# The scatters of counts beside the third graph layer's product wait for that product's progress

## The chip, the cores and the metric

The kernel runs on one core of a Trainium2 chip. The metric is the time of one execution on the device in microseconds, the median of several runs. One more execution was taken with the hardware profiler on; its trace is what the rows below come from.

## What is computed

A network of four layers over a graph with 3125 nodes of 256 features and 53125 edges (25000 random pairs in both directions and one loop per node, sorted by target). Each layer is a graph operation and a feed-forward one, both added to x. Cut to what this case touches:

```python
# third graph layer: aggregation with edge weights
h = x @ weight_l
msgs = edge_val[:, None] * h[edge_col]
agg = segment_sum(msgs, edge_row, num_segments=3125)
out = agg + bias_l + x @ weight_r + bias_r

# fourth graph layer: two graph convolutions over the same edges
s, d = concatenate([src, loop]), concatenate([dst, loop])
dinv = rsqrt(segment_sum(ones_like(d), d, num_segments=3125))
out = segment_sum((x @ W)[s] * (dinv[s] * dinv[d])[:, None], d, 3125) + b
```

## The kernel before

The layers run one after the other. Each is made of blocks; in a block the five engines have a program each, and no engine starts the next block before all have finished the last. Nodes are kept in 26 tiles of 128, edges in 416 tiles of 128 (`ET`).

The third and fourth graph layers do their segment sums as products with a dense matrix. For that, two tables in device memory are filled edge by edge long before they are read: `edge_weights` (f32, by `place_weights`, L150) with the weights for the third layer, and `edge_counts` (bf16, by `place_counts`, L141) with the number of repeats of an edge for the fourth. A tile of 128 edges is one indirect DMA that GpSimd issues and that writes 128 single elements to computed addresses, a scatter. At most four scatters of a table are in flight: each has one of four semaphores (`LANES`, L136), and a scatter waits until the one four before it has landed. The scatters are spread by hand over the blocks in which GpSimd has little to do; `COUNTED` (L831) says how many counts are placed by the end of which block:

```python
COUNTED = (97, 302, 336, 348, 374)
```

Counts 0 to 96 are placed in the feed-forward block before, 97 to 301, that is 205 scatters, in the block `weighted_products` (L2770), 302 to 335 in the block after it, `layer2_sums` (L2870), the others later. Nobody reads `edge_counts` before the fourth graph layer.

Some scatters of weights are issued by `place_weights_beside` (L159), which makes scatter t wait for a semaphore of the block's product first, so that the scatters are spread over it: those in the first feed-forward layer (L872) and in the second graph layer's sum.

`weighted_products` multiplies the normalized nodes with the matrix of weights. TensorE walks over a list `order` of 56 steps, `(h, s)`: two halves of the target nodes, and 28 slices of 128 sources in each. In a step it does 8 matmuls (L2841) of 128 rows by 391 columns in f32, 2 halves of the features by 4 pieces of the targets, one for each bank of PSUM; a bank collects over the 28 slices of a half and is copied out by ScalarE (L2856) at the end of it. Only the last matmul of a step increments the semaphore `used`. SyncE loads the 782 KB of weights of a step (L2794) into one of six buffers and waits on `used` for a free one. The sources' slices 25 to 27 beyond the nodes' own tiles come from four gathers that GpSimd issues first (L2824), after the table of nodes has been stored. VectorE and ScalarE normalize the nodes in the block's first 15 us (`StepNorm`) and then have next to nothing to do.

In the trace each f32 matmul of this block leaves two records of matmul and two of weight load.

Of the kernel before, what the change touches and what calls it, by code (L numbers as in the profile page):

```python
# [135 lines left out]
def landed(eng, lanes, t):  # L136

    eng.wait_ge(lanes[t % LANES], 16 * (t // LANES + 1))


def place_counts(nc, g, pool, lo, hi):  # L141

    for t in range(lo, hi):
        if t >= LANES:
            landed(pool, g.counts_in, t - LANES)
        nc.gpsimd.indirect_dma_start(g.counts, bass.IndirectOffsetOnAxis(ap=g.cell[:, t:t + 1].bitcast(U32), axis=0),  # L146
                                     g.repeats[:, t:t + 1], None).then_inc(g.counts_in[t % LANES], 16)


def place_weights(nc, g, pool, lo, hi):  # L150

    for t in range(lo, hi):
        if t >= LANES:
            landed(pool, g.weights_in, t - LANES)
        nc.gpsimd.indirect_dma_start(g.weights, bass.IndirectOffsetOnAxis(ap=g.share_cell[:, t:t + 1].bitcast(U32), axis=0),  # L155
                                     g.shares[:, t:t + 1], None).then_inc(g.weights_in[t % LANES], 16)


def place_weights_beside(nc, g, pool, lo, hi, signal, first, steps):  # L159

    for t in range(lo, hi):
        pool.wait_ge(signal, first + (t - lo) * steps // (hi - lo))
        place_weights(nc, g, pool, t, t + 1)


def layer_norm(nc, g, table, meanwhile=None, arrived=None):
# [664 lines left out]
COUNTED = (97, 302, 336, 348, 374)  # L831
# [5 lines left out]
def layer0_ffn(nc, g, a, table):  # L837

    scratch = nc.dram_tensor("score_scratch", (ROWS,), F32).ap()
    with ExitStack() as stack:  # L840
# [8 lines left out]
        with ExitStack() as s2:  # L849
# [12 lines left out]
            @block.gpsimd  # L862
            def _(pool):

                nc.gpsimd.affine_select(out=before[:, :], in_=g.ones[:, :], compare_op=ALU.is_gt, fill=0.0, base=0,
                                        pattern=[[-1, P]], channel_multiplier=1).then_inc(passed, 1)

                place_weights(nc, g, pool, 0, PLACED[0])
                for t in range(0, NT):
                    front.normed(pool, t)  # L870
                    nc.gpsimd.tensor_tensor(g.x[:, t, :], g.x[:, t, :], g.xn[:, t, :], ALU.add).then_inc(passed, 1)
                place_weights_beside(nc, g, pool, PLACED[0], PLACED[1], hidden, 5, NF * (ROWS // G))  # L872
# [638 lines left out]
def weighted_sum(nc, g, kept, weight, bias):  # L1511

    with ExitStack() as stack:
# [25 lines left out]
        @block.gpsimd  # L1539
        def _(pool):  # L1540
            nc.gpsimd.memset(no_edges[:, :], 0.0).then_inc(blank, 1)
            for t in range(ST):
                nc.gpsimd.tensor_tensor(g.x[:, t, :], g.x[:, t, :], bias[:, :], ALU.add).then_inc(biased, 1)
            place_weights_beside(nc, g, pool, PLACED[3], PLACED[4], summed, 1, PAIRS)
# [1225 lines left out]
def weighted_products(nc, g, a, table, bias, pairs):  # L2770
# [5 lines left out]
    with ExitStack() as stack:  # L2776
# [3 lines left out]
        stored, listed, fetched, used, done, lifted, numbered, biased, held = (sem(n) for n in (  # L2780
            "rows_stored", "listed", "fetched", "used", "done", "lifted", "numbered", "biased", "held"))
# [4 lines left out]
        first = a.dst_row[1:1 + ET * P].rearrange("(t n) -> t n", n=P)[:, 0:2]  # L2786
        rest = NODES - whole * P
        order = [(h, s) for h in range(2) for s in range(WT)]

        @block.sync  # L2790
        def _(sp):
            def load(i):
                h, s = order[i]
                sp.dma_start(weights[:, i % S, :], by_row[s * P:(s + 1) * P, h * half:(h + 1) * half]).then_inc(loaded[i % S], 16)  # L2794

            for lane in g.weights_in:
                sp.wait_ge(lane, 16 * (ET // LANES))
            for i in range(S):
                load(i)
            for dst, src in pairs:  # L2800
                sp.dma_start(dst, src).then_inc(held, 16)
            sp.wait_ge(numbered, 2)
            sp.dma_start(idx[rest:P, 0, :], first[0:P - rest, :]).then_inc(listed, 16)
            for k in range(1, WT - whole):
                lo = P - rest + (k - 1) * P
                n = min(P, ET - lo)
                sp.dma_start(idx[0:n, k, :], first[lo:lo + n, :]).then_inc(listed, 16)
            norm.normed(sp, norm.BY_ACT - 1)
            norm.normed(sp, NT - 1)
            sp.dma_start(table.rearrange("(t p) d -> p t d", p=P), g.xn[:, :, :]).then_inc(stored, 16)  # L2810
            for i in range(S, len(order)):
                sp.wait_ge(used, i - S + 1)
                load(i)
            sp.wait_ge(held, 16 * len(pairs))

        @block.gpsimd
        def _(pool):
            nc.gpsimd.memset(idx[:, :, :], 0).then_inc(numbered, 1)
            pool.wait_ge(numbered, 1)
            nc.gpsimd.iota(idx[0:rest, 0, :], [[0, 2]], base=whole * P, channel_multiplier=1).then_inc(numbered, 1)  # L2820
            pool.wait_ge(stored, 16)
            pool.wait_ge(listed, 16 * (WT - whole))
            for k in range(WT - whole):
                nc.gpsimd.indirect_dma_start(extra[:, k, :], None, table,  # L2824
                                             bass.IndirectOffsetOnAxis(ap=idx[:, k, 0:1].bitcast(U32), axis=0)).then_inc(fetched, 16)
            place_counts(nc, g, pool, COUNTED[0], COUNTED[1])

        @block.tensor
        def _(pe):
# [581 lines left out]
```

## Time and profile before

| | us |
|---|---|
| median of the timed runs | 3591.89 |
| lowest and highest of three | 3591.84, 3598.81 |
| span of the profiled execution | 4271.3 |
| mean clock granted to TensorE in it | 0.856 |
| block `weighted_products` in it, first matmul to last | 2588.9 to 3104.8 |

The profiled execution takes longer than the timed ones. Times of a row are its own, in us from the span's start. In the rows PE is TensorE's matmuls, PEld its weight loads, DVE VectorE, ACT ScalarE, POOL GpSimd, SP SyncE; PEclk is the granted clock as a share of the full 2.4 GHz, so 0.50 is the lower level, 1.2 GHz. "issue" is idle time for which the profile shows no event that was waited for.

### The profile page before, as it was taken

The numbers are of one execution on the slowest core, as the hardware profiler recorded it, in microseconds if no ns is written. First come the engines' busy times: TensorE is split into PE (matmuls) and PEld (weight loads), VectorE is DVE, ScalarE is ACT, GpSimd is POOL, SyncE is SP. The second block draws the span as 40 slices with busy tenths as digits, with TensorE's granted clock in tenths as the row PEclk, the third lists the DMA queues.
The fourth block names the chain that finished last, engine by engine and source line by source line (L and its number), as shares of the span: only waits on it lengthen the run. The fifth ranks groups of instructions, "written<-read, shape, count | busy, mean of one in ns | idle before, by whom it ended". The sixth has DMA issues, their size and how long they took to land. (4 is left out here: it accounts for less than half of the span.)

```text
span 4271.3 us, 47439 instructions
## 1 busy us (share of the span) xinstructions
PE 3169.9 (74%) x14365; PEld 2194.5 (51%) x14365; DVE 1967.2 (46%) x4724; ACT 1137.9 (27%) x2521; POOL 2014.5 (47%) x2031
## 2 busy tenths in 40 slices
PE   4777777976888888459955886228975885998966
PEld 3565655854444445248843553114553553445856
DVE  5444446924666666899961342000024336023332
ACT  3444441221222222249931110000022221012310
POOL 5666664664555555675555553770035552000032
PEclk9888988987888988669977998558987997999978
DMA  5455452004766766248831225004313114452434
GB/s 176 159 160 160 160 159 94 1 13 142 197 198 192 202 186 199 68 151 271 281 117 63 93 65 197 23 15 136 128 45 128 52 52 141 151 198 86 152 125 137
DMA packets 281656, 563.05 MB, mean 132 GB/s; under 512 B 61793, under 2 KB 184101, under 8 KB 280774
## 3 DMA queue, kind: packets, MB, share of 16 engines
q1 hardware_dynamic: 200070, 404.27, 28.4%
q0 software_dynamic: 81344, 155.76, 13.4%
q8 instruction: 127, 2.08, 0.2%
q14 instruction: 115, 0.94, 0.1%
HBM read 381.99 MB, written 177.86 MB: 131 GB/s over the span
## 5 line engine op out<-in xcount | busy, mean ns | idle before, releaser
L1282 PE MATMUL bank<-layer_gnn_h_nodes,layer_gnn_s_onehot_t 128*128 x1664 | 547.9, 457 | 110.4 <-issue 73.5
L146 POOL DMA_INDIRECT edge_counts<-repeats,count_cell x416 | 408.1, 981 | 360.8 <-SPq L2872 226.5
L155 POOL DMA_INDIRECT edge_weights<-shares,share_cell x416 | 463.5, 1114 | 240.8 <-issue 91.9
L1234 POOL DMA_INDIRECT layer_gnn_s_rows<-gat_rows,src_cols x416 | 401.6, 965 | 355.2 <-DMA kept_rows<-layer_gnn_s_rows 211.3
L527 POOL DMA_INDIRECT layer_gnn_sum_rows<-xn_rows,src_cols x416 | 417.8, 1004 | 199.1 <-issue 110.8
L2841 PE MATMUL bank<-layer_gnn_b_weights,xn_nodes 128*128 128x391 f32 x768 | 300.7, 534 | 205.1 <-issue 173.3
L1282 PEld LDWEIGHTS bank<-layer_gnn_h_nodes,layer_gnn_s_onehot_t 128*128 128x128 f32 x1664 | 317.7, 212 | 208.8 <-issue 135.8
L2841 PEld LDWEIGHTS bank<-layer_gnn_b_weights,xn_nodes 128*128 128x128 f32 x768 | 155.5, 203 | 349.8 <-issue 225.1
L1292 ACT ACTIVATE layer_gnn_s_enc<-bank 128x256 f32<-128x256 f32 x416 | 154.7, 384 | 592.1 <-PE bank L1275 345.7
L590 PE MATMUL bank<-layer_gnn_sum_onehot,layer_gnn_sum_rows 128*128 128x256 f32 x832 | 296.8, 442 | 2.0 <-issue 1.8
L1311 DVE TENSOR_TENSOR layer_gnn_s_mix<-bank,layer_gnn_s_enc 128x256 f32<-128x256 f32 x416 | 176.0, 423 | 257.9 <-PE bank L1282 124.2
L2924 DVE TENSOR_TENSOR x_nodes<-x_nodes,bank 128x256 f32<-128x256 f32 x25 | 10.4, 417 | 556.8 <-issue 501.6
L1554 PE MATMUL bank<-layer_gnn_w_onehot,layer_gnn_w_part 128*128 128x256 f32 x832 | 251.6, 385 | 20.0 <-DVE layer_gnn_w_part L1599 19.8
L3254 PE MATMUL bank<-layer_gnn_gcn_sum_counts,layer_gnn_parts 128*128 128x512 bf16 (+1 forms) x1050 | 226.9, 379 | 8.4 <-DVE layer_gnn_parts L2962 7.1
L615 ACT ACTIVATE layer_gnn_sum_onehot<-layer_gnn_sum_dist,ones 128x384 f32<-128x384 f32 x208 | 126.3, 608 | 321.1 <-remote 182.6
L721 DVE TENSOR_TENSOR edge_sums_turned<-edge_sums_turned,bank 128x512 f32 x208 | 141.7, 681 | 129.3 <-PE bank L591 62.9
L591 PEld LDWEIGHTS bank<-layer_gnn_sum_onehot,layer_gnn_sum_rows 128*128 128x128 f32 x832 | 179.6, 216 | 34.5 <-issue 3.5
L2148 PE MATMUL bank<-layer_ffn_e_w,layer_ffn_e_ht 128*128 128x256 f32 x512 | 127.9, 410 | 69.3 <-DVE layer_ffn_e_y L2204 49.7
L591 PE MATMUL bank<-layer_gnn_sum_onehot,layer_gnn_sum_rows 128*128 128x128 f32 x832 | 178.0, 299 | 1.5 <-issue 1.4
L1303 DVE TENSOR_TENSOR layer_gnn_s_onehot_t<-layer_gnn_s_dst_across,edge_sums 128x256 f32<-128x256 int32 x416 | 172.8, 416 | 4.0 <-DMA layer_gnn_s_edge_attr<-attr_parts 4.0
L553 PE MATMUL bank<-layer_gnn_sum_key_line,layer_gnn_sum_ones 3*128 3x512 bf16 x104 | 43.9, 422 | 173.0 <-DVE layer_gnn_sum_same L684 125.0
L3254 PEld LDWEIGHTS bank<-layer_gnn_gcn_sum_counts,layer_gnn_parts 128*128 128x128 bf16 x1050 | 103.2, 99 | 131.1 <-issue 10.6
(645 smaller groups left out, 6077.7 us busy)
## 6 DMA issues: line engine op xcount, KB each, us to landing
kept_rows<-layer_gnn_s_rows SPq DMA_DIRECT2D x104, 512.0 KB
layer_gnn_w_rows<-kept_rows SPq DMA_DIRECT2D x104, 512.0 KB
edge_weights<-layer_gnn_sum_zeros SPq DMA_DIRECT2D x56, 800.0 KB
layer_gnn_gcn_sum_counts<-edge_counts SPq DMA_DIRECT2D x50, 896.0 KB
layer_gnn_b_weights<-edge_weights SPq DMA_DIRECT2D x56, 782.0 KB
layer_gnn_s_dst_across<-in_dst_row SPq DMA_DIRECT2D x104, 256.0 KB
edge_counts<-layer_gnn_w_no_edges SPq DMA_DIRECT2D x25, 896.0 KB
layer_ffn_e_w<-in_l1f_w SPq DMA_DIRECT2D x16, 1024.0 KB
```

The lines of the kernel that those rows point to most:

```text
L146: nc.gpsimd.indirect_dma_start(g.counts, bass.IndirectOffsetOnAxis(ap=g.cell[:, t:t + 1].bitcast(U32), axis=0), g.repeats[:, t:t + 1], Non ...
L155: nc.gpsimd.indirect_dma_start(g.weights, bass.IndirectOffsetOnAxis(ap=g.share_cell[:, t:t + 1].bitcast(U32), axis=0), g.shares[:, t:t + 1 ...
L527: nc.gpsimd.indirect_dma_start(rows[:, t % U, :], None, table, bass.IndirectOffsetOnAxis(ap=g.srcc[:, t:t + 1].bitcast(U32), axis=0)).then ...
L590: nc.tensor.matmul(sums(p)[:, c, :], rows[:, t % U, c * P:(c + 1) * P], onehot[:, p % 4, P:3 * P], start=True, stop=False)
L591: last = nc.tensor.matmul(sums(p)[:, c, 0:P], rows[:, (t - 1) % U, c * P:(c + 1) * P], onehot[:, p % 4, 0:P], start=False, stop=True)
L1234: nc.gpsimd.indirect_dma_start(rows[:, t % U, :], None, htable, bass.IndirectOffsetOnAxis(ap=g.srcc[:, t:t + 1].bitcast(U32), axis=0)).the ...
L1282: last = nc.tensor.matmul(g.ps[4 + t % 4][:, 0:D + HEADS], onehot_t[:, t % 4, k, :], hflat[:, ds(w * AW + (k * AW + HEADS), D + HEADS)], s ...
L1303: nc.vector.tensor_tensor(onehot_t[:, t % 4, :, :], dst[:, t // Q % PARTS, t % Q * P:(t % Q + 1) * P].unsqueeze(1).to_broadcast([P, 2, P]) ...
L1311: nc.vector.tensor_tensor(mix[:, t % 4, :], g.ps[4 + t % 4][:, 0:D], enc[:, t % 4, :], ALU.mult).then_inc(mixed, 1)
L1554: nc.tensor.matmul(sums(p)[:, c, :], part[:, p % 4, 1, c * P:(c + 1) * P], onehot[:, p % 4, P:3 * P], start=True, stop=False)
L2841: last = nc.tensor.matmul(g.ps[4 * c + j][:, 0:w], rows, weights[:, i % S, j * w:(j + 1) * w], start=(s == 0), stop=(s == WT - 1))
L3254: last = nc.tensor.matmul(g.ps[b][:, 0:cells(b)], parts[:, k, s * P:(s + 1) * P], counts[:, s % S, b * 512:b * 512 + cells(b)], start=(s = ...
```

## The change

A new function `place_counts_beside` does for the counts what `place_weights_beside` does for the weights, and `weighted_products` calls it in place of `place_counts`:

```diff
+def place_counts_beside(nc, g, pool, lo, hi, signal, first, steps):
+
+    for t in range(lo, hi):
+        pool.wait_ge(signal, first + (t - lo) * steps // (hi - lo))
+        place_counts(nc, g, pool, t, t + 1)
@@ weighted_products, @block.gpsimd
-            place_counts(nc, g, pool, COUNTED[0], COUNTED[1])
+            place_counts_beside(nc, g, pool, COUNTED[0], COUNTED[1], used, 4, len(order) - 6)
```

`used` is the semaphore of finished steps, `len(order) - 6` is 50. So the first scatter waits until 4 steps of the product are done, and the last of the 205 until 4 + 204 x 50 // 205 = 53 are. The other lines of the program, and the order of instructions on every engine, stay as they are (line numbers behind the new function grow by 7).

On GpSimd this is where the scatters start in `weighted_products`, before:

```order
L2820 IOTA layer_gnn_b_idx 53x2 [waits layer0_gnn_sum_gathered3]
L2824 DMA layer_gnn_b_extra<-xn_rows,layer_gnn_b_idx 128x256 [waits layer0_gnn_ln_scaled,layer0_gnn_ln_normed]
L2824 DMA layer_gnn_b_extra<-xn_rows,layer_gnn_b_idx 128x256 x3
L146 DMA edge_counts<-repeats,count_cell 11468800x1 [waits counts_in1]
L146 DMA edge_counts<-repeats,count_cell 11468800x1 [waits counts_in2]
L146 DMA edge_counts<-repeats,count_cell 11468800x1 [waits counts_in3]
L146 DMA edge_counts<-repeats,count_cell 11468800x1 [waits counts_in0]
```

and after (a semaphore that is used again under another name is printed with its first name; `layer0_gnn_sum_gathered0` is `used` here):

```order
L2827 IOTA layer_gnn_b_idx 53x2 [waits layer0_gnn_sum_gathered3]
L2831 DMA layer_gnn_b_extra<-xn_rows,layer_gnn_b_idx 128x256 [waits layer0_gnn_ln_scaled,layer0_gnn_ln_normed]
L2831 DMA layer_gnn_b_extra<-xn_rows,layer_gnn_b_idx 128x256 x3
L146 DMA edge_counts<-repeats,count_cell 11468800x1 [waits counts_in1,layer0_gnn_sum_gathered0]
L146 DMA edge_counts<-repeats,count_cell 11468800x1 [waits counts_in2,layer0_gnn_sum_gathered0]
L146 DMA edge_counts<-repeats,count_cell 11468800x1 [waits counts_in3,layer0_gnn_sum_gathered0]
L146 DMA edge_counts<-repeats,count_cell 11468800x1 [waits counts_in0,layer0_gnn_sum_gathered0]
```

Nothing has moved; each scatter of the block has one more semaphore to wait for.

## Rows read from the trace of the kernel before

**Rows 1.** The page: span, and TensorE's busy tenths and clock in 40 slices.
```profile
span 4271.3 us, 47439 instructions
...
PE   4777777976888888459955886228975885998966
...
PEclk9888988987888988669977998558987997999978
```

**Rows 2.** Busy time by stretches, columns in the first line, x counts instructions.
```profile
core 0: us, PE busy (x) PEld busy (x) DVE busy (x) ACT busy (x) POOL busy (x), PEclk, DMA share, GB/s
50.00:650.00 600.00, 439.58 (x2730) 356.33 (x2730) 289.47 (x538) 278.08 (x628) 402.47 (x409) 0.87 0.50 160
1050.00:1750.00 700.00, 588.82 (x1989) 338.82 (x1989) 459.18 (x1624) 147.98 (x398) 375.93 (x390) 0.87 0.68 194
...
2589.00:2657.00 68.00, 68.00 (x200) 38.91 (x201) 17.99 (x54) 6.73 (x14) 31.79 (x34) 0.97 0.69 240
2657.00:2902.00 245.00, 72.13 (x91) 25.51 (x90) 0.00 (x0) 0.00 (x0) 168.40 (x176) 0.51 0.08 20
2902.00:3105.00 203.00, 202.37 (x606) 115.22 (x606) 0.00 (x0) 7.64 (x16) 0.00 (x0) 0.99 0.42 135
...
750.00:900.00 150.00, 144.82 (x658) 126.49 (x658) 109.07 (x197) 46.89 (x105) 93.50 (x97) 0.98 0.02 1
```

**Rows 3.** TensorE's timeline in the product: start, length, what, idle before and releaser.
```profile
start us, us, engine line op out<-in xcount [idle before <-releaser]
2588.86 68.36 PE L2841 MATMUL bank<-layer_gnn_b_weights,xn_nodes 128*128 128x391 f32 x200 [31.82 <-DMA layer_gnn_b_weights<-edge_weights]
...
2682.62 0.81 PE L2841 MATMUL bank<-layer_gnn_b_weights,xn_nodes 128*128 128x391 f32 x1 [1.99 <-issue]
2685.42 0.81 PE L2841 MATMUL bank<-layer_gnn_b_weights,xn_nodes 128*128 128x391 f32 x1 [1.99 <-issue]
...
2902.42 33.83 PE L2841 MATMUL bank<-layer_gnn_b_weights,xn_nodes 128*128 128x391 f32 x94 [0.59 <-issue]
...
2957.15 126.56 PE L2841 MATMUL bank<-layer_gnn_b_weights,xn_nodes 128*128 128x391 f32 x384
3083.55 21.23 PE L2841 MATMUL bank<-layer_gnn_b_weights,layer_gnn_b_extra 128*128 128x391 f32 x64
```

**Rows 4.** GpSimd's timeline beside the product: the first scatter, and the last two.
```profile
2618.08 0.99 POOL L146 DMA_INDIRECT edge_counts<-repeats,count_cell  x1 [0.30 <-issue]
...
2877.50 0.96 POOL L146 DMA_INDIRECT edge_counts<-repeats,count_cell  x1 [0.30 <-issue]
2878.76 0.96 POOL L146 DMA_INDIRECT edge_counts<-repeats,count_cell  x1 [0.30 <-issue]
```

**Rows 5.** TensorE's timeline in the block after it, from 3122 on.
```profile
3133.73 0.47 PE L2888 MATMUL bank<-identity,xn_nodes 128*128 128x128 f32 x1
3136.53 0.37 PE L2888 MATMUL bank<-identity,xn_nodes 128*128 128x128 f32 x1 [2.33 <-issue]
3139.33 0.59 PE L2899 MATMUL bank<-layer_gnn_wl,edge_sums_turned 128*128 128x256 f32 x1 [2.42 <-issue]
3141.43 0.59 PE L2899 MATMUL bank<-layer_gnn_wl,edge_sums_turned 128*128 128x256 f32 x1 [1.51 <-issue]
...
3154.52 2.07 PE L2899 MATMUL bank<-layer_gnn_wl,edge_sums_turned 128*128 128x256 f32 x4
```

**Rows 6.** DMA queues from 2580 to 3110: packets, MB, share of 16 engines.
```profile
q8 instruction: 7, 0.11, 0.1%
```

**Rows 7.** The page's groups: the gathers of the first graph layer.
```profile
L527 POOL DMA_INDIRECT layer_gnn_sum_rows<-xn_rows,src_cols x416 | 417.8, 1004 | 199.1 <-issue 110.8
```

**Rows 8.** GpSimd's timeline, paced scatters of weights in the first feed-forward layer.
```profile
807.94 0.96 POOL L155 DMA_INDIRECT edge_weights<-shares,share_cell  x1 [0.30 <-issue]
811.65 1.00 POOL L155 DMA_INDIRECT edge_weights<-shares,share_cell  x1 [2.76 <-PE bank L901]
812.96 0.95 POOL L155 DMA_INDIRECT edge_weights<-shares,share_cell  x1 [0.30 <-issue]
```

## The prediction

> **What bounds the kernel now.** I began with the page: the profiled execution spans 4271.3 us, the three timed runs have a median of 3591.89 us, so the profiled one is 679 us longer. That gap has to be kept in mind through everything below. The reader is to see two digits in the page's slices [rows 1]: slices 26 and 27 are the only ones in which TensorE is under 30% busy at the lower of its two clocks while vector and scalar engines do nothing at all. They lie in the third graph layer's product, and that is where the change works. No engine bounds the whole span; stage follows stage behind barriers, so only this stage's end matters.
>
> I then read busy time by stretches [rows 2]. From 2589 to 2657 TensorE is 100% busy, from 2902 to 3105 again (202.4 of 203 us). Between, from 2657 to 2902, it has 91 matmul records in 245 us. The product's timeline shows how [rows 3]: one record every 2.8 us, each put down to "issue", that is, waiting for nothing the profile can see; before and after, a step of the product (8 matmuls, 16 records) takes 126.56 / 24 = 5.27 us, or 21.23 / 4 = 5.31 us. GpSimd's timeline beside it [rows 4]: 205 scatters of counts from 2618.08 to 2878.76, one every 1.26 us, hardly ever waiting. The slow pace begins 39 us after the first scatter and ends about 23 us after the last. The same thing happens once more: with the 34 scatters of the next block TensorE falls to one record in 2.1 to 2.8 us from 3122 on, and returns to full pace at 3154.5 [rows 5]. So scatters at GpSimd's full rate and a slow TensorE go together in the profiled execution. Unslowed, the product would have ended at 2588.9 + 56 x 5.27 = 2884.0; it ended at 3083.55 + 21.23 = 3104.8. The stretch costs **221 us of the profiled span**. The whole case turns on one question: does a timed run pay it too?
>
> **Is the slow stretch in the timed runs?** Against: (a) The pace does not depend on the work. A record of 391 columns, of 256 and of 128 all come 2.8 us apart [rows 3, 5], and nothing in the program ties a single matmul to a scatter: only the eighth of a step increments a semaphore. A contention for data would scale with columns. (b) Data can't be short: the DMA engines are 8% busy there (20 GB/s) and TensorE waits for its weights once, at the start [rows 2, 3]. The instruction queue fetched 7 packets with 0.11 MB over the stage, about 64 B for each of its 1792 matmul and weight-load records, so nothing is fetched twice [rows 6]. What is left is something paid per instruction, and keeping a record of each instruction and each transfer is what only the profiled execution does. (c) The 679 us must come from somewhere. In the stretches I can bound, little can go: the first layer's gathers cannot go below 409 x 1.26 = 515 of 600 us (85 to gain), the edge scores not below TensorE's 589 of 700 (111), the first feed-forward layer not below 145 of 150 (5) [rows 2, 7]. With 2902 to 3105 (nothing to gain) that makes 201 us in 1653. If the slow stretch counts as extra, the other 2373 us have to give 679 - 201 - 221 = 257 us, 11%; if it is in the timed runs too, they have to give 478 us, 20%. The first is easier to believe. (d) GpSimd's scatters end at 2879.7, just inside the unslowed product's 2884.
>
> For: the profile shows no record being waited for, and (c) uses GpSimd's 1.26 us as a floor, of which 0.30 are "issue" and may themselves be the profile's.
>
> The Trainium skill's page "SBUF — State Buffer" (section "SBUF: two separate sides") says that engine ports and DMA ports are apart and that a DMA and a compute operation can't slow each other. The trace can neither confirm nor refute the rule for these scatters; by it, pacing them frees nothing in a timed run, 0 us, which speaks against a gain from this change.
>
> **The change, part by part.** Nothing is added to compute or to move; the same 205 scatters stand in the same order on GpSimd's queue, each with one more semaphore to wait for: scatter i of 205 waits until 4 + (50 i) // 205 steps are done.
> - *Do the waits bind in a timed run?* Steps take 5.27 us, so the schedule lets 4.1 / 5.27 = 0.778 scatters pass per us; GpSimd's own rate is 1 / 1.26 = 0.794. At the first scatter (2618.08) (2618.1 - 2588.9) / 5.27 = 5.5 steps are done, where the schedule asks for 4, so it starts 8 scatters behind the limit and gains 0.016 x 258 = 4 in the whole phase. The waits hardly ever bind. If a timed run's GpSimd is quicker (0.96 us, the busy part alone), they do: then the scatters end when step 53 does, 2588.9 + 53 x 5.27 = 2868, plus 4 scatters, 2873: still 11 us inside the product. Nothing is queued behind them on GpSimd but the block's end, and nobody reads the counts before the last graph layer. Cost 0.
> - *What does a wait that is already met cost?* The scatters of shares in the first feed-forward layer have just such a wait each, and come 1.26 us apart like those without [rows 4, 8]. Under 0.01 us each, 205 x 0.01 = 2 us, covered by the 4 us by which GpSimd ends ahead of the product. Cost 0; without that cover 2 us.
> - *What does TensorE gain?* In the timed runs between 0 and 221 us. I take 0, by (a) to (c).
> - *The other 34 scatters* (next block) keep their place and rate. 0.
>
> Sum for the timed runs: 0, so 3591.9, and I put 3591 for it. In the **profiled** execution the waits do bind once TensorE slows: GpSimd then stops with it, and TensorE gets the gaps. The nearest row is the paced stretch from 750 to 900: 97 scatters and 658 records in 150 us, TensorE 145 us busy at clock 0.98 [rows 2]: 0.65 scatters per us leave 4.4 records per us untouched. Here it would be up to 0.78 per us beside 3.0 records. I expect steps of 5.3 to 6.3 us, 56 x 5.3 to 6.3 = 297 to 353 us in place of 516, so a profiled span shorter by 160 to 220 us, while the median stays.
>
> **Rivals.**
> 1. *The timed runs have the whole slow stretch.* Then the gain above is real: 3592 minus 160 to 220 is 3372 to 3432, say 3400. For it: the trace shows the slowdown plainly and no cause in the recording. Against: (a) to (c). 0.17. The Trainium skill's page "NOTIFIC — the notification-queue block" (section "10. Constraints, capacities, measured rates") says that emitting an instruction's record costs the engine zero cycles, which would make the stretch real and the time this rival's; its section "7.1 Overflow" knows a mode in which a full queue stalls the engine that writes, which would make it the profile's own, and the time my forecast's. No row tells the two apart.
> 2. *The timed runs have a part of it.* GpSimd's flood slows semaphores or issue a little without records too. Of 221 us, 5 to 25% is 11 to 55 us: 3537 to 3581. 0.09.
> 3. *Slower: the added wait lengthens each scatter.* It decides from the point at which 205 scatters overrun the product, (2884 - 2879.7) / 205 = 0.02 us each. If the gap of 0.30 us became 0.40, the phase would end 205 x 0.10 - 4 = 16 us after the product: 3608; if it doubled, 205 x 0.30 - 4 = 57 us: 3649. Against it stand the paced scatters at 1.26 us [rows 8]. 0.10, with smaller overruns beside it.
> 4. *The change does nothing even in the profile*: the limit lies 8 scatters ahead and the rate is 98% of the old one. TensorE slows as before, but then the limit is reached within some 10 scatters, so I give this little weight; the timed runs would stay at 3592 all the same. It is inside the forecast.
>
> **How the numbers follow.** About 0.2% (7 us) is what a measurement of this kernel can tell from no change; the three runs themselves are 3591.84 to 3598.81. Forecast 3591, within 0.2%: 0.62 (with rival 4). Rival 1 0.17, rival 2 0.09, and 0.02 for a small gain from an unseen overlap: faster 0.28. Rival 3 with its smaller forms: slower 0.10. The range runs from 3540 (most of rival 2) to 3608 (rival 3 at 0.10 us more per scatter); it leaves out rival 1 and the long overruns, 0.2 together.
>
> **What would show it right or wrong.** In the changed kernel's profile: records in the product about 0.33 us apart throughout, few or no "issue" waits of 2 us, the product's length 297 to 353 us, scatters still 1.26 us apart within a burst with waits for TensorE between bursts, the last one before the product's end; the stretch from 3122 to 3154 just as slow as now, only earlier. If the profiled span falls by some 200 us and the median by nothing, the slow stretch was the profile's own. If both fall by as much, step (a) to (c) is wrong and rival 1 right. If scatters are further apart than 1.26 us inside a burst and the block ends with GpSimd, it is rival 3.

## The result, and the profile after

The changed kernel takes 3605.3 us (11 runs, 3599.1 to 3608.4), the kernel before beside it 3595.5 us (11 runs): ratio 1.0031, 95% interval 1.0023 to 1.0039. It is slower by 9.8 us between the medians, by some 11 us (8 to 14) by the ratio. The forecast was 3591 us and no change. Two executions of the kernel before that took far longer than all others beside them (4465.3 and 7233.8 us, clocks 0.763 and 1.0) enter no ratio.

One thing has to be said before any row is read. The kernel before was seen at two levels in this study: on chips 5, 10 and 14 and beside the result (that chip is not on record) the medians of its timed runs are 3592 to 3596 us, on chips 0 and 7 they are 4274 and 4303 us. I call these the short and the long level. The trace read ahead of the prediction (4271.3 us) shows the long level, the timed runs beside it the short one. The trace of the changed kernel shows the short one (3600.4 us), so its difference to rows 1 to 5 is mostly not the change. A second trace of the kernel before at the short level, taken as the first experiment, is what it has to be read against.

The page of the changed kernel: span, TensorE's busy tenths and its clock in 40 slices, as in [rows 1].

```profile
span 3600.4 us, 47644 instructions
...
PE   4887887996999999079977987998589859999696
...
PEclk9999998997999999589988998999789979999898
```

The same lines of the kernel before at the short level:

```profile
span 3593.7 us, 47439 instructions
...
PE   4878877995999999179986986999589869999696
```

There is no stretch of TensorE under 30% in the product (slices 25 to 28 here) any more, but there is none in the kernel before either. What differs is the end of the block. TensorE's timeline, the product's last stretches and the next block's first matmuls, in the changed kernel ([rows 3] are the like):

```profile
start us, us, engine line op out<-in xcount [idle before <-releaser]
2181.65 128.08 PE L2848 MATMUL bank<-layer_gnn_b_weights,xn_nodes 128*128 128x391 f32 x384 [37.39 <-DMA layer_gnn_b_weights<-edge_weights]
...
2457.03 21.23 PE L2848 MATMUL bank<-layer_gnn_b_weights,layer_gnn_b_extra 128*128 128x391 f32 x64
2493.87 1.94 PE L2895 MATMUL bank<-identity,xn_nodes 128*128 128x128 f32 x8 [15.60 <-PEq L2783]
```

and in the kernel before at the short level:

```profile
2183.78 128.88 PE L2841 MATMUL bank<-layer_gnn_b_weights,xn_nodes 128*128 128x391 f32 x384 [38.23 <-DMA layer_gnn_b_weights<-edge_weights]
...
2459.97 21.23 PE L2841 MATMUL bank<-layer_gnn_b_weights,layer_gnn_b_extra 128*128 128x391 f32 x64
2486.21 1.94 PE L2888 MATMUL bank<-identity,xn_nodes 128*128 128x128 f32 x8 [5.00 <-PEq L2776]
```

The product itself is as long in both (296.6 and 297.4 us). TensorE then waits 5.00 us for the next block in the one and 15.60 in the other. GpSimd's timeline tells why. Changed kernel, the block's first scatter, its last, and the next block's first ([rows 4] are the like):

```profile
2210.93 0.99 POOL L146 DMA_INDIRECT edge_counts<-repeats,count_cell  x1 [0.30 <-issue]
...
2484.80 0.95 POOL L146 DMA_INDIRECT edge_counts<-repeats,count_cell  x1 [0.31 <-issue]
2494.47 0.96 POOL L146 DMA_INDIRECT edge_counts<-repeats,count_cell  x1 [8.72 <-SPq L2879]
```

Kernel before, short level:

```profile
2213.07 0.99 POOL L146 DMA_INDIRECT edge_counts<-repeats,count_cell  x1 [0.30 <-issue]
...
2477.14 0.96 POOL L146 DMA_INDIRECT edge_counts<-repeats,count_cell  x1 [0.30 <-issue]
2486.82 0.95 POOL L146 DMA_INDIRECT edge_counts<-repeats,count_cell  x1 [8.72 <-SPq L2872]
```

In both, TensorE's first matmul of the next block comes 9.07 us after the start of GpSimd's last scatter (2493.87 - 2484.80, 2486.21 - 2477.14). That fits a block that GpSimd ends, in the kernel before too, though its last scatter starts 4 us before the product is over; two runs below try it. And the 205 scatters take 2484.80 - 2210.93 = 273.9 us with the change and 2477.14 - 2213.07 = 264.1 us without it: 9.8 us, as much as the medians differ.

### The profile page after: what moved, and what is told of

The parts are those of the page before. It is cut to its first block and busy times, and to the rows that moved or that the text cites. A ratio compares the mean times of both kernels' runs of the same rounds, so it can differ in the third digit from the quotient of the medians.

```text
span 3600.4 us, 47644 instructions
## 1 busy us (share of the span) xinstructions
PE 2979.0 (83%) x14365; PEld 2110.7 (59%) x14365; DVE 1972.7 (55%) x4724; ACT 1154.6 (32%) x2521; POOL 2015.6 (56%) x2031
## 3 DMA queue, kind: packets, MB, share of 16 engines
q0 software_dynamic: 81344, 155.76, 15.4%
## 5 line engine op out<-in xcount | busy, mean ns | idle before, releaser
L1289 PE MATMUL bank<-layer_gnn_h_nodes,layer_gnn_s_onehot_t 128*128 x1664 | 484.4, 414 | 0.9 <-DVE layer_gnn_s_onehot_t L1310 0.2
L597 PE MATMUL bank<-layer_gnn_sum_onehot,layer_gnn_sum_rows 128*128 128x256 f32 x832 | 276.9, 416 | 97.2 <-DMA layer_gnn_sum_rows<-xn_rows,src_cols 86.9
L1289 PEld LDWEIGHTS bank<-layer_gnn_h_nodes,layer_gnn_s_onehot_t 128*128 128x128 f32 x1664 | 283.3, 190 | 79.7 <-issue 4.0
L2848 PE MATMUL bank<-layer_gnn_b_weights,xn_nodes 128*128 128x391 f32 x768 | 254.6, 493 | 37.4 <-DMA layer_gnn_b_weights<-edge_weights 37.4
L1561 PE MATMUL bank<-layer_gnn_w_onehot,layer_gnn_w_part 128*128 128x256 f32 x832 | 250.1, 382 | 15.1 <-DVE layer_gnn_w_part L1606 14.5
L2848 PEld LDWEIGHTS bank<-layer_gnn_b_weights,xn_nodes 128*128 128x128 f32 x768 | 146.0, 190 | 145.7 <-DMA layer_gnn_b_weights<-edge_weights 37.8
L597 PEld LDWEIGHTS bank<-layer_gnn_sum_onehot,layer_gnn_sum_rows 128*128 128x128 f32 x832 | 134.8, 202 | 124.3 <-issue 81.7
L2931 DVE TENSOR_TENSOR x_nodes<-x_nodes,bank 128x256 f32<-128x256 f32 x25 | 10.5, 421 | 324.5 <-PE bank L2909 324.5
L598 PEld LDWEIGHTS bank<-layer_gnn_sum_onehot,layer_gnn_sum_rows 128*128 128x128 f32 x832 | 168.0, 202 | 25.9
L1562 PEld LDWEIGHTS bank<-layer_gnn_w_onehot,layer_gnn_w_part 128*128 128x128 f32 x832 | 158.7, 191 | 21.6
L609 ACT ACTIVATE layer_gnn_sum_dist<-iota_row,ayer_gnn_sum_minus_local 128x128 f32<-128x128 f32 (+1 forms) x416 | 166.0, 447 | 13.8 <-DVE ayer_gnn_sum_minus_local L631 7.9
```

The lines of the kernel that those rows point to most:

```text
L597: nc.tensor.matmul(sums(p)[:, c, :], rows[:, t % U, c * P:(c + 1) * P], onehot[:, p % 4, P:3 * P], start=True, stop=False)
L598: last = nc.tensor.matmul(sums(p)[:, c, 0:P], rows[:, (t - 1) % U, c * P:(c + 1) * P], onehot[:, p % 4, 0:P], start=False, stop=True)
L1289: last = nc.tensor.matmul(g.ps[4 + t % 4][:, 0:D + HEADS], onehot_t[:, t % 4, k, :], hflat[:, ds(w * AW + (k * AW + HEADS), D + HEADS)], s ...
L1561: nc.tensor.matmul(sums(p)[:, c, :], part[:, p % 4, 1, c * P:(c + 1) * P], onehot[:, p % 4, P:3 * P], start=True, stop=False)
L2848: last = nc.tensor.matmul(g.ps[4 * c + j][:, 0:w], rows, weights[:, i % S, j * w:(j + 1) * w], start=(s == 0), stop=(s == WT - 1))
```

## The experiments at the short level

In all of them the ratio is to the kernel before on the same chip in the same minutes. "Block" is the time from the product's first matmul to the next block's first, "phase" that from the start of the block's first scatter of counts to the start of its last, "gap" TensorE's idle time before the next block's first matmul. The last three columns are in us, from one trace of each kernel.

| | added waits | ratio (95%) | phase | block | TensorE's gap |
|---|---|---|---|---|---|
| before, again | 0 | 1.0000 (0.9991 to 1.0008) | 264.1 | 302.4 | 5.0 |
| the change | 205 | 1.0031 (1.0023 to 1.0039) | 273.9 | 312.2 | 15.6 |
| all waits already met | 205 | 1.0037 (1.0024 to 1.0049) | 273.9 | 312.2 | 14.4 |
| waits 3 to 9 steps earlier | 205 | 1.0031 (1.0019 to 1.0043) | 272.9 | 311.2 | 14.5 |
| landing first | 205 | 0.9999 (0.9989 to 1.0008) | 264.1 | 302.3 | 4.5 |
| a wait at every eighth | 26 | 1.0023 (1.0014 to 1.0032) | 267.0 | 305.4 | 8.2 |
| before, 8 scatters fewer | 0 | 0.9991 (0.9982 to 1.0001) | 254.4 | 298.0 | 0.8 |
| the change, 8 fewer | 197 | 1.0000 (0.9991 to 1.0009) | 261.8 | 299.4 | 1.3 |
| landing first, 8 fewer | 197 | 0.9991 (0.9982 to 1.0000) | 255.2 | 297.9 | 0.8 |
| before, 8 in flight | 0 | 0.9975 (0.9966 to 0.9985) | 257.9 | 297.8 | 0.8 |
| the change, 8 in flight | 205 | 0.9973 (0.9962 to 0.9983) | 257.6 | 297.7 | 0.8 |

**The kernel before, again.** No edit.

> The kernel before, unchanged, for a second trace of it and as a control of the comparison: ratio 1.000. Theory A (the block's end waits for GpSimd): in a profiled execution without the slow stretch the product ends about 2478 + shift, the last of the 205 scatters starts before the product's last matmul or at most 5 us behind it, and TensorE's first matmul of the next block follows 10 to 12 us earlier after the product's end than the 15.6 us it takes in the changed kernel. Theory B (something else in the span got slower): the distance from the product's last matmul to the next block's first is the same 15.6 us here, and the 10 us lie elsewhere.

Measured: the gap is 5.0 and not 15.6 us, theory A. But the block waits for GpSimd already here: its last scatter's start is followed by 9.07 us of block end, and the product is over after 4.07 of them.

**Do the waits cost because they bind?** Two edits of the call:

```diff
-            place_counts_beside(nc, g, pool, COUNTED[0], COUNTED[1], used, 4, len(order) - 6)
+            place_counts_beside(nc, g, pool, COUNTED[0], COUNTED[1], used, 4, 0)
```

> The changed kernel, but each of the 205 added waits asks only for 4 finished steps, which are done before the first scatter. If the instruction of a wait costs time by itself (205 x 0.05 us = 10 us), this is as slow as the change, ratio to before about 1.003. If the waits cost only where they hold a scatter back, it is as fast as before, 1.000.

```diff
-            place_counts_beside(nc, g, pool, COUNTED[0], COUNTED[1], used, 4, len(order) - 6)
+            place_counts_beside(nc, g, pool, COUNTED[0], COUNTED[1], used, 1, len(order) - 12)
```

> The changed kernel with the schedule 3 to 9 steps ahead (first wait for 1 step, last for 44 in place of 53). If holding back by steps is what costs, the waits bind no longer, and GpSimd ends as in the kernel before: ratio 1.000. If a wait costs by itself, 1.003, as in the run with all waits met.

Measured: 1.0037 and 1.0031, phases of 273.9 and 272.9 us. No wait for the product holds anything back; that the wait is there costs as much as the whole change. Pacing itself does nothing at this level.

**Which wait, and how many.** The traces show what a second wait does here: of the two waits of a scatter one becomes an instruction of its own, and it is the one written second. In `place_counts_beside` the step is waited for first and the landing (inside `place_counts`) second. So the change takes the wait for the landing off the scatter:

```
before          scatter [waits counts_in1]
change          wait counts_in1; scatter [waits used]
landing first   wait used; scatter [waits counts_in1]
```

The trace has these extra instructions on GpSimd's queue, 205 more with the change at the line of `landed` (before, then change; 17 ns each); with the landing first that line is back at 266, and the 205 are at the line of the added wait (third row):

```profile
L138 POOLq EVENT_SEMAPHORE  x266: 17/17/17, 647.2 to 1835.1; - x133
...
L138 POOLq EVENT_SEMAPHORE  x471: 17/17/17, 644.1 to 2481.9; - x157
...
L170 POOLq EVENT_SEMAPHORE  x205: 17/17/17, 2207.9 to 2473.0; - x103
```

The edit that swaps the two, and nothing else (shortened: `scatter_counts` stands for the scatter as `place_counts` issues it, without its own wait):

```diff
     for t in range(lo, hi):
-        pool.wait_ge(signal, first + (t - lo) * steps // (hi - lo))
-        place_counts(nc, g, pool, t, t + 1)
+        landed(pool, g.counts_in, t - LANES)
+        pool.wait_ge(signal, first + (t - lo) * steps // (hi - lo))
+        scatter_counts(nc, g, pool, t)
```

> The changed kernel with the two waits of a scatter in the other order: first for the scatter four before it, then for the product's step. The theory now: every scatter has one instruction more on GpSimd (205 in all), and the time is lost where the landing of an earlier scatter comes late. If it matters which of the two waits rides on the scatter itself, this is faster than the change (scatter phase under 270 us against 273.9, ratio nearer to 1.000). If only the number of instructions counts, it is the same: 273.9 us and 1.003.

Measured: 0.9999. The same 205 instructions more, the same conditions, and no cost. So my first reading, that the number of instructions costs, fell; it is the wait for the landing that must not stand alone. The groups of GpSimd's scatters in the phase (count, busy and mean, idle before them) show it for the kernel before, the change, all waits met, and landing first, in this order:

```profile
L146 POOL DMA_INDIRECT edge_counts<-repeats,count_cell x205 | 196.7, 959 | 68.6 <-issue 57.3 <-DMA edge_counts<-repeats,count_cell 11.4
...
L146 POOL DMA_INDIRECT edge_counts<-repeats,count_cell x205 | 196.2, 957 | 78.9 <-issue 52.9 <-PE bank L2848 16.4 <-DMA edge_counts<-repeats,count_cell 9.6
...
L146 POOL DMA_INDIRECT edge_counts<-repeats,count_cell x205 | 196.7, 960 | 78.4 <-issue 51.6 <-PE bank L2848 15.4 <-DMA edge_counts<-repeats,count_cell 11.5
...
L171 POOL DMA_INDIRECT edge_counts<-repeats,count_cell x205 | 196.3, 958 | 69.1 <-issue 54.5 <-DMA edge_counts<-repeats,count_cell 10.9 <-PE bank L2850 3.7
```

A scatter takes 0.96 us in all; what grows is the idle time before it, 68.6 to 78.9 us. The reader should not take "PE bank L2848 16.4" at its word: with all waits for the product met long before, it is still 15.4. The profile names the last event before a start, and the landing wait had no row of its own here. The loss sits in single pauses, most of them four or eight scatters apart, and not in 0.05 us at each. Beyond the 0.305 us that stand before every scatter, the timelines have 18 pauses with 6.2 us in all in the kernel before and 32 with 16.3 us in the change (idle times over 0.35 us counted). So more scatters are held, and each for longer. In the changed kernel:

```profile
2225.63 0.96 POOL L146 DMA_INDIRECT edge_counts<-repeats,count_cell  x1 [0.64 <-PE bank L2848]
...
2236.40 0.95 POOL L146 DMA_INDIRECT edge_counts<-repeats,count_cell  x1 [0.98 <-PE bank L2848]
```

Fewer waits, by

```diff
-        pool.wait_ge(signal, first + (t - lo) * steps // (hi - lo))
+        if (t - lo) % 8 == 0:
+            pool.wait_ge(signal, first + (t - lo) * steps // (hi - lo))
```

> The changed kernel with the added wait at every eighth scatter only, 26 waits in place of 205. If the added instructions are the cost (9.8 us for 205 in the traces, 0.048 us each), 26 cost 1.2 us: ratio 1.0003, scatter phase about 265.3 us. If pacing by steps as such costs, it stays at 1.003.

Measured: 1.0023, where I expected 1.0003. In its trace the phase is 2.9 us longer than before and the block 3.0 us, so a good third of the timed 8 us (5 to 11) is found in the block. The trace's other 5.3 us lie ahead of the block, whose first matmul starts at 2189.1 in place of 2183.8 us, and there the two kernels do not differ; whether the timed runs lose them there too is not known. With 26 waits each costs 0.11 us in the trace, twice the 0.048 us of the change. A price per wait is the wrong picture, which fits pauses at late landings, but 2 us or more of the timed loss stay open.

**Does GpSimd end the block?** Take 8 scatters out of it, in the kernel before and in the change:

```diff
-COUNTED = (97, 302, 336, 348, 374)
+COUNTED = (97, 294, 328, 340, 366)
```

> The kernel before with 8 scatters fewer in the product's block (197 in place of 205); the 8 are issued by the last of the stages instead, beside the third layer's experts. Theory: GpSimd ends the block, 9.07 us after its last scatter starts. Then the phase is 10 us shorter, but TensorE can start the next block no earlier than about 0.8 us after its own end, 4.2 us before now: a gain of about 4 us, ratio 0.999, and the gap of TensorE between the blocks falls from 5.0 to 0.8 us. If the product ends the block, the gap stays at 5.0.

> The changed kernel with the same 8 scatters fewer in the block. If the change costs what it does because GpSimd ends the block, 8 x (1.26 + 0.05) = 10.5 us come back of the 14.8 us by which TensorE's gap is above 0.8: ratio to before about 1.000, gap 4 to 5 us in place of 15.6. If the added cost lies elsewhere, the ratio stays at 1.003.

Measured: in the kernel before the gap falls to 0.84 us, which is what a block change costs TensorE when nobody is late, and the block is 4.5 us shorter:

```profile
2463.79 21.23 PE L2841 MATMUL bank<-layer_gnn_b_weights,layer_gnn_b_extra 128*128 128x391 f32 x64
2485.86 1.06 PE L2888 MATMUL bank<-identity,xn_nodes 128*128 128x128 f32 x8 [0.84 <-PEq L2776]
```

In the timed runs that is 3 us, at the edge of what can be told from nothing. In the changed kernel the gap goes from 15.6 to 1.3 us, where 4 to 5 were expected (the phase is 12.1 us shorter and not 10.5, and the block end 8.4 us and not 9.07), and the ratio from 1.0031 to 1.0000. So the change's cost reaches the end only because the block ends with GpSimd.

**Late landings.** If what hurts is a landing that comes late behind a wait of its own, it must vanish when a scatter waits for the one eight before it instead of four. The edit holds for counts and weights alike:

```diff
-LANES = 4
+LANES = 8
```

> The kernel before with eight scatters in flight in place of four, for counts and weights alike, so that a scatter waits for the one eight before it (10.1 us earlier instead of 5.05, against landings of 2.1 to 6.2 us). Theory: the pauses in the product's block (264.1 us for 205 scatters, where 204 x 1.26 = 257.5 would do) are late landings. Then the phase falls to 258 us, its last scatter starts at least 10.5 us before the product's end, and TensorE's gap between the blocks falls from 5.0 to 0.8 us: ratio 0.999 or lower, since the other scatters pause less too. If the pauses come from something else (the loads of weights slowing GpSimd itself), the phase stays at 264.

> The changed kernel with eight scatters in flight. Theory: the change costs because it moves the wait for a landing from the scatter onto an instruction of its own ahead of it, and a landing that comes late then holds the scatter back longer. With eight in flight no landing is late, so the 205 separate waits cost nothing: phase 258 to 262 us, same as the kernel before with eight, ratio 0.999. If separate waits cost whatever the landings do, the phase stays some 10 us longer than there, and the ratio is 1.001 to 1.003.

These two fell on a chip at the long level and are told below, and so did the next pair. At the short level they were taken on chip 14:

> The kernel before with eight scatters in flight. Where the kernel before takes 3594 us: the phase's pauses are gone, 258 us, gap of TensorE 0.8 us, ratio 0.997 to 0.999. Where it takes 4270 to 4300: 1.003 to 1.006.

> The changed kernel with eight scatters in flight. Where the kernel before takes 3594 us: if the separate waits for a landing cost only when the landing is late, the phase is 258 to 262 us and the ratio that of the kernel before with eight; if always, 0.003 more. Where it takes 4270 to 4300: 0.958 to 0.961.

Measured: phases of 257.9 and 257.6 us, 204 x 1.262 = 257.4 being the least possible, ratios 0.9975 and 0.9973. The same groups for the two:

```profile
L146 POOL DMA_INDIRECT edge_counts<-repeats,count_cell x205 | 196.7, 959 | 62.5 <-issue 62.5
...
L146 POOL DMA_INDIRECT edge_counts<-repeats,count_cell x205 | 196.4, 958 | 62.5 <-issue 52.4 <-DMA edge_counts<-repeats,count_cell 5.8 <-PE bank L2848 4.3
```

62.5 us of idle time in both, which is 205 x 0.305: not one pause is left, and the change's 205 separate waits cost nothing. That settles it at this level: the pauses are waits for landings, and the change makes them more and longer. The kernels with eight in flight gain 9 to 10 us, though, and the block gives only 4.7 of them; the rest lies outside it, where the edit reaches all other scatters. In the changed kernel the landings took

```profile
DMA to landing us min/median/max: 2.1/2.4/6.2
```

while four scatters last 5.05 us, so only the slow ones matter. That they are slow because they share the DMA engines with the 782 KB of weights of every step is likely and not shown for a single landing. It fits that in the slow stretch of [rows 2], where the DMA engines are 8% busy, 176 scatters have 54.6 us of idle time before them, 0.31 each, so next to no pause. Why a landing behind its own instruction delays its scatter by more is not shown; that the scatter can only be prepared after the separate wait has passed would fit, and was not tried.

## The experiments at the long level

Eight scatters in flight were timed on both chips where the kernel before takes 4274 and 4303 us, the change itself and landing first on the second of them.

> The change itself, once more. Beside the last two runs the kernel before took 4274 us, beside all others 3594: there are two groups of chips or conditions, and TensorE's slow stretch next to the scatters belongs to the long one, timed runs included. If the kernel before takes about 3594 us here: ratio 1.003. If it takes about 4274: the product's block shrinks from 516 to 320 to 335 us, ratio 0.957 to 0.965. If the slow stretch were the profile's alone, the ratio would be 1.003 in both.

> The changed kernel with the two waits in the other order (first the landing, then the step). Where the kernel before takes 3594 us: ratio 1.000 again. Where it takes 4274 us: as the change, 0.957 to 0.965, since the pace is the same.

> The kernel before with eight scatters in flight. Where the kernel before takes 3594 us: the pauses of the phase (6.2 us beyond 1.26 us each, after the first six) are gone, phase 258 us, gap of TensorE 0.8 us, ratio 0.997 to 0.999. Where it takes 4274: 1.003, as measured.

> The changed kernel with eight scatters in flight. Where the kernel before takes 3594 us: if separate waits for a landing cost only when the landing is late, as fast as the kernel before with eight, 0.997 to 0.999 and a phase of 258 to 262 us; if they cost always, 0.003 more. Where it takes 4274: 0.958, as measured.

| | kernel before, us | this, us | ratio (95%) | block, us |
|---|---|---|---|---|
| before, 8 in flight | 4274.0 | 4289.5 | 1.0031 (1.0008 to 1.0055) | 530.5 |
| the change, 8 in flight | 4274.0 | 4097.6 | 0.9584 (0.9554 to 0.9614) | 327.5 |
| the change | 4303.3 | 4125.9 | 0.9581 (0.9552 to 0.9609) | 336.2 |
| landing first | 4303.3 | 4116.4 | 0.9576 (0.9545 to 0.9608) | 333.9 |
| before, 8 in flight | 4303.3 | 4327.1 | 1.0057 (1.0033 to 1.0082) | 530.6 |
| the change, 8 in flight | 4303.3 | 4133.5 | 0.9612 (0.9587 to 0.9638) | 331.0 |

One execution of each kernel "this" is the profiled one; it takes as long as the others (the change 4126.0 us against 4108.0 to 4129.0). So the slow stretch of [rows 2, 3] is real where it occurs, and there the change takes 4.2% off. The changed block ends with GpSimd here too: TensorE's first matmul of the next block comes 6.7 us after the product and 9.08 us after the start of the last scatter. The ratios came as expected for the change and for landing first; eight in flight came out worse on the second chip than the 1.003 and 0.958 of the first had led me to expect. The stretches of the product in the changed kernel at this level, to be read against the third and fourth of [rows 2] (columns as there):

```profile
core 0: us, PE busy (x) PEld busy (x) DVE busy (x) ACT busy (x) POOL busy (x), PEclk, DMA share, GB/s
2611.00:2650.00 39.00, 39.00 (x112) 22.23 (x113) 17.98 (x54) 6.73 (x14) 10.17 (x11) 0.94 0.92 337
2650.00:2930.00 280.00, 261.34 (x755) 144.56 (x755) 0.00 (x0) 3.98 (x8) 183.22 (x192) 0.97 0.40 127
```

755 records in 280 us where [rows 2] have 91 in 245. The timelines show the change doing what it says. TensorE slows after some 20 scatters with hardly a pause:

```profile
2727.28 0.49 PE L2848 MATMUL bank<-layer_gnn_b_weights,xn_nodes 128*128 128x391 f32 x1 [2.16 <-issue]
2728.71 0.81 PE L2848 MATMUL bank<-layer_gnn_b_weights,xn_nodes 128*128 128x391 f32 x1 [0.94 <-issue]
2730.11 0.81 PE L2848 MATMUL bank<-layer_gnn_b_weights,xn_nodes 128*128 128x391 f32 x1 [0.59 <-issue]
2731.51 17.71 PE L2848 MATMUL bank<-layer_gnn_b_weights,xn_nodes 128*128 128x391 f32 x47 [0.59 <-issue]
```

and GpSimd's next scatter then waits 3.2 us (the releaser's name is an old name of `used`), after which TensorE is at full pace again for 17.7 us:

```profile
2727.60 0.95 POOL L146 DMA_INDIRECT edge_counts<-repeats,count_cell  x1 [0.30 <-issue]
2731.77 0.95 POOL L146 DMA_INDIRECT edge_counts<-repeats,count_cell  x1 [3.22 <-DMA layer_gnn_sum_rows<-xn_rows,src_cols]
```

A pause of three scatters is enough at this point to end what otherwise lasts 245 us. It may not be enough later: in the trace of before TensorE is back at full pace only 23.7 us after the start of the last of the 205 scatters (2902.42 - 2878.76, [rows 3, 4]), and 6.6 us after that of the last of the 34 in the next block ([rows 5]):

```profile
3147.89 0.95 POOL L146 DMA_INDIRECT edge_counts<-repeats,count_cell  x1 [0.30 <-issue]
```

The longer the scatters have run, the longer TensorE takes to recover, as if something had piled up; what it is, no row shows. Eight in flight without the change cost 0.3 and 0.6% (1.0031 and 1.0057, both clear of 1), and the order of the two waits makes no difference (0.9576 against 0.9581).

## A version that is at least as good at both levels

> A version meant to beat both: the changed kernel with the landing waited for first, and with 8 scatters fewer in the block. Where the kernel before takes 3594 us: the phase is some 254 us, TensorE's gap between the blocks 0.8 us, ratio 0.999 like the kernel before with 8 fewer. Where it takes 4270 to 4300 us: 0.955 to 0.958, since the pace is as in the change.

Measured at the short level only: 0.9991 (0.9982 to 1.0000), 3587.6 us. The change with eight scatters in flight is better and was timed at both: **0.9973 at the short level (3582.9 us), 0.9584 and 0.9612 at the long one**. Against the change alone it is 0.6% faster at the short level (each against the kernel before on its own chip). On the one chip at the long level where both were timed it is 0.3% behind (0.9612 against 0.9581), with intervals that overlap. At the short level the gain is that of the eight in flight: without the change they give the same (0.9975).

## Why the prediction was right or wrong

- *The slow stretch is not in the timed runs.* Right for the level at which the kernel was timed first, wrong as a statement on the kernel. The step that failed is (c): the 679 us between profiled span and median are not what a profile adds, but the distance between the two levels. The second profiled execution of the kernel before took 3595.5 us in all against a median of 3594.0: the profile adds nothing one could measure. Step (b), that what is paid per instruction must be the keeping of records, falls with it: the timed runs at 4274 and 4303 us keep none. Step (a), that the pace hardly depends on the columns, stands; what causes it is open. One of the floors in (c) was none either. In the edge scores TensorE's busy time was taken for it, 589 of 700 us; the whole stage takes 736 us in the trace read ahead and 550 at the short level, for the same records, at clocks of 0.86 and 1.00:

```profile
1013.00:1749.00 736.00, 618.15 (x2079) 355.68 (x2079) 478.27 (x1689) 154.59 (x416) 396.78 (x411) 0.86 0.68 193
...
883.00:1433.00 550.00, 543.51 (x2080) 320.37 (x2080) 485.42 (x1691) 159.88 (x416) 395.94 (x412) 1.00 0.88 258
```

  Of the 678 us between the two traces of the kernel before, 405 lie ahead of the product's block, 214 in it and 58 behind it: the long level is more than this one stretch, and the change touches only the 214. Rival 1 was right at the long level, with its size: 160 to 220 us were given, 177 measured (4303.3 - 4125.9), and a step of 5.3 to 6.3 us against 329.5 / 56 = 5.9.
- The Trainium skill's page "NOTIFIC — the notification-queue block" (section "10. Constraints, capacities, measured rates"), by which a record costs the engine nothing, agrees with these runs: 3595.5 us profiled, 3594.0 not. The Trainium skill's page "SBUF — State Buffer" (section "SBUF: two separate sides"), by which a DMA and a compute operation can't slow each other, would have the pacing free nothing; at the long level it freed 177 us. The rule may still be right about the ports, since no row shows which resource the two share.
- *The waits hardly ever bind: 0.* Right at the short level, as the run with all waits met shows.
- *A wait that is already met costs under 0.01 us.* This is the step that failed and turned the result from no change to slower. It was read off the paced scatters of [rows 8], which run where the DMA engines are 2% busy (the last of [rows 2]) and where no wait is put down to a landing. Beside the loads of weights the same construction costs 9.8 us for 205, 0.048 us each. The row was the nearest one and still the wrong one: the price hangs on what the wait that is moved off the scatter is waiting for.
- *GpSimd ends 4 us inside the product, and that covers it.* Wrong in the size of the cover, which was below zero. As the prediction measures it, from the last scatter's end to the product's, it is 3.1 us in the kernel before at the short level and not 4: the phase and the product are both a little longer there. What the prediction left out is the block end, 9.07 us from the last scatter's start. With it the block ends 4.2 us later than the product alone would let it (5.00 - 0.84). No row ahead of the prediction showed that, because at the long level GpSimd was done 226 us before the product.
- *Rival 3* is what happened: the added wait lengthens the scatters and the block ends with GpSimd. It was priced at 0.10 us each with a cover of 4 us, 16 us; measured are 0.048 us each without a cover, 10 us. Its point of decision, 0.02 us, should have been zero.

## What to carry to other kernels

A second wait on an instruction is not free even when it is met: look at which of the two then stands alone, and write the one that may come late first, so that it rides on the instruction. If an engine issues DMAs up to the end of a block, count its block end too (9 us here). And when a profiled span and a median differ by far more than a per cent, ask for a second trace before explaining the difference: trace and timed runs may come from different levels of the machine.

## What the runs showed of the hardware that was not expected

- The same program takes 3592 to 3596 us (medians) in four sets of runs and 4274 and 4303 us in two; no set changed its level while it was timed. Each set ran on one chip, and none of the chips 0, 5, 7, 10 and 14 was timed a second time, so whether the level belongs to the chip or to the time of the run is open.
- At the long level back-to-back scatters slow TensorE to one matmul record in 2.1 to 2.8 us, of 391, 256 or 128 columns alike ([rows 3, 5]). It begins 39 us after the first of 205 scatters and 16 us after the first of 34, and ends 23.7 and 6.6 us after the start of the last one; 3.2 us without a scatter ended it early on. At the short level 205 scatters at full rate do nothing to it: 896 records in 298 us.

```profile
2184.00:2482.00 298.00, 297.21 (x896) 170.35 (x896) 17.99 (x54) 14.69 (x30) 200.54 (x209) 0.99 0.51 163
```

- The end of this block costs TensorE 0.84 us when GpSimd's last scatter started some 10 us or more before the product's end, and otherwise ends 9.07 us after the start of that scatter (8.4 to 9.4 in other runs).
